# Routed rows in a two-expert layer: sorting row numbers instead of rows, fetching by them and scattering the results

## The chip, the cores and the metric

The kernel runs on one core of one Trainium2 chip. The metric is the device time of one launch in microseconds. Three runs of the kernel before took 1113.02, 1115.05 and 1116.56, median 1115.05. One more execution was profiled; all rows below are from it.

## The reference

x has 4 sequences of 1024 tokens of 256 numbers, T = 4096 tokens in all. Both branches start from the same normalised rows xn; the results are multiplied and added to x. All is float32.

```python
xn = layernorm(x)                                     # over 256
# branch 1: differential attention, 8 heads, head size 32, causal
q, k, v = xn @ wq.T, xn @ wk.T, xn @ wv.T             # q, k: two maps per head
attn = softmax(q0 k0 / sqrt(32)) - lmbda * softmax(q1 k1 / sqrt(32))
o = attn @ v                                          # per head
o = o * rsqrt(mean(o * o, over groups of 4) + 1e-6) * (1 - L_INIT)
s = o @ wo.T
# branch 2: 8 experts, the best 2 of each token
logits = xn @ router.T + router_bias
top_vals, top_idx = top_k(logits, 2);  top_w = softmax(top_vals)
gate, up = split(xn @ gate_up[e] + bias[e])           # 256 -> 2 * 256
glu = min(gate, 7) * sigmoid(1.702 * gate)
y[e] = ((clip(up, -7, 7) + 1) * glu) @ down[e] + down_bias[e]
g = silu(sum over the 2 experts of top_w * y[e])
out = x + s * g
```

## The kernel before

The program has four stages, each a block in which every engine runs its own list of instructions; at the exit of a block all five engines meet. The order inside a list is written out by hand, and engines wait on counting semaphores.

*Projections.* Eight chunks of 512 tokens. DVE normalises, PE turns the rows and makes q, k (as high and low parts, `PARTS`, stored by SP to `q_parts` and `k_parts`, L313), v and the logits. POOL makes constants at the start: masks, identity, a tile of zeros (L264), counters (L269 to L281); PE's and DVE's lists wait for `consts_done` 6. SP writes the zeros to `xs_dram` in eight DMAs (L303). DVE ranks the logits of each batch and, after the last, works out the routing (L497 to L548): a scan over the 32 tiles of tokens (six doublings, L503 to L507), the tokens and tiles of each expert, the first slot of each, the expert of each of 72 slot tiles (`expert_rows`), the slot of each token's two choices (`slot_of`) and their weights. The steps of `low_parts` (L433) stand between those of the routing in DVE's list.

*Attention.* 16 iterations of two heads, each eight frames (p = 0 to 7) of a long and a short block of queries. PE scores, DVE takes maxima and combines the two maps (L1050, L1100), ACT takes exponentials and copies. SP loads the q and k of the next head while the present one is scored (L782, L162, L163) and, in iterations 0 to 7, the weights of one expert. POOL copies v (L813), keeps the results (`keep_rows`, L826; two frames of slack to ACT) and sorts the experts' inputs: it loads two tiles of xn rows an iteration (L832), copies their slots (L833) and scatters each tile twice to `xs_dram` (L844), 1 KB a row, and waits for the scatters at the iteration's end. Rows of the slots that no token has stay zero.

*Experts.* 72 tiles of 128 slots, all buffers double. SP loads a tile of `xs_dram` when PE has turned the tile two before (L1184). In step n PE does the gate and up product of tile n+1 (L1242), turns the input of n+2 (L1228), does the down product of n-1 (L1268) and turns the activation of n (L1255). DVE adds the bias (L1359), limits the gate (L1369), multiplies (L1378), limits up (L1381), makes `act_in` (L1387) and the output `ys` (L1399). ACT copies and takes tanh, and stores `ys` plainly to `ys_dram` (L1330). POOL has nothing to do.

*Last stage.* Eight chunks of 512 tokens (b, h). POOL copies a chunk's slots and weights and gathers its 8 tiles of `ys_dram` rows (L1507, 4 tiles times 2 choices) into `yg`. ACT squares the attention results (L1571), scales the first choice (L1580, waits for the gathers), takes root and tanh (L1589, L1594). DVE in `normalise` copies a divisor (L1631), sums squares, adds the second choice (L1653), inverts the root (L1659) and scales to `On` (L1672); in `finish` of the chunk before it multiplies and adds (L1678, L1684, L1688). PE turns `On` and multiplies by wo (L1544, L1553). SP loads x and stores the result.

## Time and profile before

| | |
|---|---|
| median of 3 runs | 1115.05 us |
| the profiled execution | 1113.86 us, span 1112.0 us |
| PE, DVE, ACT, POOL busy | 941.5, 938.0, 776.8, 221.7 us |
| mean granted clock of PE | 0.949 |
| DMA | 178.11 MB, mean 160 GB/s |
| read from and written to HBM | 108.56 and 69.21 MB |

The span runs from the first to the last instruction; what the execution has around it is 1.9 us. Busy times overlap. An engine that is busy the whole of a stage sets its pace; where none is, a chain of waits does, and then the row of the instruction that is waited for tells more than the sum. A row of the timeline gives start, duration, engine, line, operation, output from inputs and, in brackets, how long the engine had stood idle and what released it.

### The profile page before, as it was taken

How to read it: one execution, taken by the hardware profiler on the slowest of the kernel's cores; microseconds unless marked ns; L12 is line 12 of the kernel's file. 1: busy time of each engine (PE TensorE's matmuls, PEld its weight loads, DVE VectorE, ACT ScalarE, POOL GpSimd, SP SyncE). 2: the span in 40 equal slices, each digit the busy share in tenths (PEclk: the TensorE clock that was granted, in tenths of full speed). 3: DMA queues.
4: the chain of work that ended last, by engine and by line, in shares of the span. 5: the costliest groups of instructions: out<-in, count | busy, mean ns of one | idle time of the engine just before them, and what ended most of it. 6: DMA issues, size and time to landing. Idle time of an engine off the chain costs nothing. (4 is left out here: it accounts for less than half of the span.)

```text
span 1112.0 us, 25771 instructions
## 1 busy us (share of the span) xinstructions
PE 941.5 (85%) x6626; PEld 659.5 (59%) x6627; DVE 938.0 (84%) x1873; ACT 776.8 (70%) x1982; POOL 221.7 (20%) x427
## 2 busy tenths in 40 slices
PE   5999858989889998988999898858999999962665
PEld 4787645666666666666666666644555555532544
DVE  6778688999999999999999999935777777754987
ACT  3554438999999999999999999942333333325663
POOL 2000001222222232222322232210000000017771
PEclk9999987999999999999999999988999999996677
DMA  7999986676786767757575665402222222223553
GB/s 258 377 366 370 328 318 137 172 183 149 172 199 165 175 157 187 184 128 165 120 159 130 139 151 128 95 15 66 80 84 77 85 80 80 80 94 96 174 182 107
DMA packets 92410, 178.11 MB, mean 160 GB/s; under 512 B 11744, under 2 KB 50144, under 8 KB 91360
## 3 DMA queue, kind: packets, MB, share of 16 engines
q1 hardware_dynamic: 74336, 147.38, 49.1%
q0 software_dynamic: 7680, 20.98, 6.5%
q10 hardware_dynamic: 10368, 9.44, 2.5%
q8 instruction: 11, 0.18, 0.1%
q14 instruction: 15, 0.12, 0.0%
HBM read 108.56 MB, written 69.21 MB: 160 GB/s over the span
## 5 line engine op out<-in xcount | busy, mean ns | idle before, releaser
L1050 DVE TENSOR_REDUCE nmax<-bank 128x1 f32<-128x1024 f32 (+3 forms) x256 | 260.4, 1017 | 4.0 <-PE bank L882 4.0
L983 ACT ACTIVATE Pr_long<-bank,nmax 128x1024 f32<-128x1024 f32 (+3 forms) x256 | 252.0, 984 | 12.2 <-DVE nmax L1050 12.1
L1010 ACT COPY AT<-bank 128x512 f32<-128x512 f32 (+3 forms) x384 | 177.0, 493 | 4.4 <-PE bank L921 2.5
L880 PE MATMUL bank<-Ks_first,Qs_first 128*128 128x512 f32 (+3 forms) x384 | 124.1, 413 | 31.1 <-ACT Pr_short L997 19.8
L1242 PE MATMUL bank<-gu_sb,xsT 128*128 x288 | 140.7, 612 | 4.8 <-DVE hid L1359 0.5
L997 ACT ACTIVATE Pr_short<-bank,nmax 128x128 f32<-128x128 f32 (+3 forms) x256 | 138.3, 540 | 8.9 <-DVE nmax L1068 1.6
L921 PE MATMUL bank<-ident,Pr_long 128*128 128x128 f32 x832 | 127.9, 281 | 18.1 <-DVE Pr_long L1100 18.1
L1100 DVE SCALAR_TENSOR_TENSOR Pr_long<-Pr_long,coef 128x1024 f32<-128x1024 f32 (+3 forms) x128 | 137.6, 1075 | 0.0
L880 PE MATMUL bank<-Ks_second,Qs_second 128*128 128x512 f32 (+3 forms) x384 | 119.4, 400 | 18.7 <-ACT Pr_short L997 18.4
L882 PE MATMUL bank<-maskb,identb 128*128 128x128 bf16 x512 | 118.1, 233 | 0.0
L921 PEld LDWEIGHTS bank<-ident,Pr_long 128*128 128x128 f32 x832 | 90.8, 143 | 31.7 <-issue 27.6
L944 PE MATMUL bank<-AT,Vj 128*32 128x128 f32 x2304 | 109.4, 279 | 0.0
L826 POOL COPY VO<-Ob 128x64 f32 (+1 forms) x128 | 30.3, 237 | 390.5 <-ACT Ob L1019 390.3
L662 PE MATMUL bank<-XNT_parts,wqk_parts 128*128 128x512 f32 x384 | 94.3, 403 | 9.7 <-DVE PARTS L433 8.3
L880 PEld LDWEIGHTS bank<-Ks_first,Qs_first 128*128 128x128 f32 x384 | 66.4, 202 | 59.3 <-ACT Pr_short L997 39.6
L880 PEld LDWEIGHTS bank<-Ks_second,Qs_second 128*128 128x128 f32 x384 | 63.5, 193 | 47.5 <-ACT Pr_short L997 39.1
L662 PEld LDWEIGHTS bank<-XNT_parts,wqk_parts 128*128 128x128 f32 x384 | 73.0, 193 | 29.5 <-issue 7.6
L882 PEld LDWEIGHTS bank<-maskb,identb 128*128 128x128 bf16 x512 | 49.9, 98 | 67.7 <-issue 49.8
L1359 DVE TENSOR_TENSOR hid<-bank,gub_sb 128x512 f32<-128x512 f32 x72 | 49.8, 692 | 35.9 <-PE bank L1242 34.3
L944 PEld LDWEIGHTS bank<-AT,Vj 128*32 128x32 f32 x2304 | 74.7, 110 | 8.8 <-issue 0.2
L1068 DVE TENSOR_REDUCE nmax<-bank 128x1 f32<-128x512 f32 (+1 forms) x128 | 79.0, 617 | 0.8 <-PE bank L882 0.6
L1242 PEld LDWEIGHTS bank<-gu_sb,xsT 128*128 128x128 f32 x288 | 49.8, 193 | 49.2 <-issue 49.2
(147 smaller groups left out, 1647.0 us busy)
## 6 DMA issues: line engine op xcount, KB each, us to landing
q_parts<-PARTS SPq DMA_DIRECT2D x32, 512.0 KB, 5.9
k_parts<-PARTS SPq DMA_DIRECT2D x32, 512.0 KB, 5.9
Qs_first<-q_parts SPq DMA_DIRECT2D x64, 256.0 KB, 6.2
Ks_first<-k_parts SPq DMA_DIRECT2D x64, 256.0 KB, 7.1
Qs_second<-q_parts SPq DMA_DIRECT2D x64, 256.0 KB, 5.9
Ks_second<-k_parts SPq DMA_DIRECT2D x64, 256.0 KB, 6.7
xs_dram<-zeros SPq DMA_DIRECT2D x8, 1152.0 KB, 8.4
xs<-xs_dram SPq DMA_DIRECT2D x72, 128.0 KB, 2.0
```

What stands on the lines that cost most here:

```text
L662: last = nc.tensor.matmul(qkbank[i % 4], wqk_parts[:, w, c, i * P:(i + 1) * P], XNT_parts[:, r, c, :], start=((c, w, r) == products[0]), s ...
L880: nc.tensor.matmul(at[:, c0:c1], Qs[head][:, m, q * P:(q + 1) * P], Ks[head][:, m, c0:c1], start=True, stop=(c1 < N))
L882: return nc.tensor.matmul(at[:, N - P:N], identb[:], maskb[:], start=False, stop=True)
L921: last = nc.tensor.transpose(tb[u % BANKS][:, i * P:(i + 1) * P], probs[:, 0, kb * P:(kb + 1) * P], ident[:])
L944: last = nc.tensor.matmul(ob[DH * g:DH * (g + 1), 0:P], Vj[head][:, kb, :], AT[unit(p, k) % 6][:, i * P:(i + 1) * P], start=first, stop=final,
L983: nc.scalar.activation(long_probs(p)[:, m, 0:N], long_slot[m][:, 0:N], ACT.Exp, bias=nmax[:, 4 * p + m:4 * p + m + 1], scale=1.0, accum_ou ...
L997: nc.scalar.activation(short_probs(p)[:, m, 0:N], short_at(p, m)[:, 0:N], ACT.Exp, bias=nmax[:, 4 * p + 2 + m:4 * p + 3 + m], scale=1.0, a ...
L1010: nc.scalar.copy(AT[u % 6][:, 0:w], tb[u % BANKS][:, 0:w]).then_inc(unit_out, 1)
L1050: nc.vector.tensor_reduce(nmax[:, 4 * p + m:4 * p + m + 1], long_slot[m][:, 0:N], AX.X, ALU.max, negate=True).then_inc(long_maxed, 1)
L1068: nc.vector.tensor_reduce(nmax[:, 4 * p + 2 + m:4 * p + 3 + m], short_slot[:, 0:N], AX.X, ALU.max, negate=True).then_inc(short_maxed, 1)
L1100: nc.vector.scalar_tensor_tensor(out=probs[:, 0, 0:N], in0=probs[:, 1, 0:N], scalar=coef[:, 2 * p + 1:2 * p + 2], in1=probs[:, 0, 0:N], op ...
L1242: last = nc.tensor.matmul(hbank[u], xsT[u][:, c, :], gu_sb[:, c, bass.ds(e, 1), :].rearrange("p o n -> p (o n)"), start=(c == 0), stop=(c ...
```

## The change

Nothing that is computed changes. Instead of the 1 KB rows, the numbers of the rows are sorted. `row_ids` holds for token t and choice k the number t + 4096 k. In eight attention iterations POOL scatters these numbers, each repeated to 64 bytes, to `ids_dram` at the token's slot; slots that nobody has hold numbers from 8192 up. SP then reads one word of each slot into `slot_rows`, and POOL makes `slot_tokens` from them (the number less 4096 once or twice). In the expert stage POOL fetches the rows of each slot tile from `xn_dram` by `slot_tokens` and scatters each result tile to `y_dram` by `slot_rows`, which lays them in token order, one plane a choice; empty slots go to 256 rows behind. SP and ACT do nothing for these transfers any more. The last stage reads `y_dram` plainly. The first tile of rows is fetched in the last attention iteration, the second at the start of the expert block, where two plain loads stand for the two first credits of `ys`.

Part of the routing moves: DVE copies the two PSUM results to SBUF (`pre`, `tot`), counts the tokens of an expert by one reduce instead of by the scan, and the scan and the slots become 14 counted steps on POOL in the first attention iteration (`route`, frames 0 to 4). Their tiles lie in the bias tile `gub_sb`, so SP waits for them before it loads the third expert. DVE's last two low parts stand before the experts' rows now. All four blocks are opened with `no_gpsimd_drain=True`.

```diff
+AHEAD = 5
...
-SORT_AT = {1: (0, 0), 2: (0, 1), 3: (1, 0), 4: (1, 1)}
+Y_ROWS = TOP_K * T + 2 * P
+ID_WORDS = 16
+SORT_ITS = T // P * TOP_K // NP
+SORT_AT = {1: (0, 1), 2: (2,), 3: (3, 4), 4: (5,), 5: (6, 7)}
...
-        xs_dram = nc.dram_tensor("xs_dram", (SLOT_TILES * P, D), F32, kind="Internal").ap()
-        ys_dram = nc.dram_tensor("ys_dram", (SLOT_TILES * P, D), F32, kind="Internal").ap()
+        ids_dram = nc.dram_tensor("ids_dram", (SLOT_TILES * P, ID_WORDS), I32, kind="Internal").ap()
+        y_dram = nc.dram_tensor("y_dram", (Y_ROWS, D), F32, kind="Internal").ap()
...
+        FREE_EXPERTS = 2
+        spare = gub_sb[:, FREE_EXPERTS:, :].rearrange("p e n -> p (e n)")
...
-            with nc.Block() as block:
+            with nc.Block(no_gpsimd_drain=True) as block:
...
-                    nc.gpsimd.memset(zeros[:], 0.0).then_inc(zeros_ready, 1)
-                    nc.gpsimd.memset(before[:], 1.0).then_inc(const_step, 1)
+                    nc.gpsimd.iota(no_rows[:], pattern=[[1, 2 * P], [0, ID_WORDS]], base=TOP_K * T, channel_multiplier=0
+                                   ).then_inc(no_rows_ready, 1)
+                    nc.gpsimd.iota(row_ids[:], pattern=[[P, NT], [T, TOP_K]], base=0, channel_multiplier=1
+                                   ).then_inc(no_rows_ready, 1)
...
-                    sp.wait_ge(zeros_ready, 1)
-                    xs_v = xs_dram.rearrange("(n p r) d -> n p (r d)", p=P, r=SLOT_TILES // NCH)
+                    sp.wait_ge(no_rows_ready, 1)
+                    sp.dma_start(ids_dram.rearrange("(q n) o -> q n o", n=2 * P), no_rows[:]).then_inc(ids_cleared, 16)
                     def chunk(b, h):
-                        sp.dma_start(xs_v[b * 2 + h], zeros[:]).then_inc(zeros_stored, 16)
...
+                    nc.vector.tensor_copy(pre, bank6[:, 0:NT * E].rearrange("p (t e) -> p t e", e=E))
+                    nc.vector.tensor_copy(tot, bank7[:, 0:NT * E].rearrange("p (t e) -> p t e", e=E))
...
-                    nc.vector.memset(run[0][:, 0:1, :], 0.0)
-                    then(nc.vector.tensor_copy(run[0][:, 1:NT, :], tot[:, 0:NT - 1, :]))
-                    src, span = 0, 1
-                    while span < NT:
-                        nc.vector.tensor_copy(run[1 - src][:, 0:span, :], run[src][:, 0:span, :])
-                        then(nc.vector.tensor_tensor(run[1 - src][:, span:, :], run[src][:, span:, :],
-                                                     run[src][:, 0:NT - span, :], ALU.add))
-                        src, span = 1 - src, 2 * span
...
+                    then(nc.vector.tensor_reduce(tokens, bank7[:, 0:NT * E].rearrange("p (t e) -> p e t", e=E), AX.X,
+                                                 ALU.add))
                     low_parts(B - 1, 1, range(QKT // 2, QKT // 2 + 2))
...
+                    nc.vector.tensor_scalar(first_slot, first, float(P), None, ALU.mult)
+                    low_parts(B - 1, 1, range(QKT // 2 + 2, QKT))
...
-                    low_parts(B - 1, 1, range(QKT // 2 + 2, QKT))
-                    then(nc.vector.tensor_tensor(run[1 - src][:], run[src][:], pre, ALU.add))
-                    then(nc.vector.tensor_tensor(run[src][:], run[1 - src][:],
-                                                 first_slot.unsqueeze(1).broadcast_to([P, NT, E]), ALU.add))
-                    for k in range(TOP_K):
-                        then(nc.vector.tensor_tensor(ck[:, k], chosen[:, k], run[src][:], ALU.mult))
-                    then(nc.vector.tensor_reduce(top[:, 3:5], ck, AX.X, ALU.add))
-                    then(nc.vector.tensor_copy(slot_of[:].rearrange("p t k -> p k t"), top[:, 3:5]))
...
-                    with sp.Fori(0, E) as it:
+                    with sp.Fori(0, FREE_EXPERTS) as it:
                         for u in range(2):
                             load(it + 1, u)
                         load_expert(it)
-                    with sp.Fori(E, NIT - 1) as it:
+                    sp.wait_ge(routed, ROUTE_OPS)
+                    with sp.Fori(FREE_EXPERTS, E) as it:
+                        for u in range(2):
+                            load(it + 1, u)
+                        load_expert(it)
+                    with sp.Fori(E, SORT_ITS + 2) as it:
+                        for u in range(2):
+                            load(it + 1, u)
+                    sp.wait_ge(ids_sorted, 16 * SORT_ITS * NP)
+                    with nc.allow_non_contiguous_dma("one word of each slot"):
+                        sp.dma_start(slot_rows[:], ids_dram[:, 0:1].rearrange("(n p) o -> p (n o)", p=P)
+                                     ).then_inc(rows_known, 16)
+                    with sp.Fori(SORT_ITS + 2, NIT - 1) as it:
                         for u in range(2):
                             load(it + 1, u)
...
+                    def double(src, span):
+                        nc.gpsimd.tensor_copy(run[1 - src][:, 0:span, :], run[src][:, 0:span, :])
+                        then(nc.gpsimd.tensor_tensor(run[1 - src][:, span:, :], run[src][:, span:, :],
+                                                     run[src][:, 0:NT - span, :], ALU.add))
...
+                    def sort_ids(it, p):
+                        if p == 0:
+                            if not isinstance(it, int):
+                                pool.wait_ge(ids_sorted, 16 * NP * (it - 1))
+                            tiles = bass.ds((it - 1) * (NP // 2), NP // 2)
+                            nc.gpsimd.tensor_copy(sort_slot[:], slot_of[:, tiles, :]).then_inc(row_slot_ready, 1)
+                            nc.gpsimd.tensor_copy(sort_id, row_ids[:, tiles, :].unsqueeze(3).broadcast_to(
+                                [P, NP // 2, TOP_K, ID_WORDS])).then_inc(row_slot_ready, 1)
+                        if p == 1:
+                            pool.wait_ge(row_slot_ready, 2 * it)
                             pool.sem_inc(scatter_begun, 1)
-                        pool.indirect_dma_start(xs_dram, bass.IndirectOffsetOnAxis(row_slot[u][:, k:k + 1], 0),
-                                                rows[u][:], None).then_inc(rows_sorted[u], 16)
+                        for n in SORT_AT.get(p, ()):
+                            i, k = n // TOP_K, n % TOP_K
+                            pool.indirect_dma_start(ids_dram, bass.IndirectOffsetOnAxis(sort_slot[:, i, k:k + 1], 0),
+                                                    sort_id[:, i, k, :], None).then_inc(ids_sorted, 16)
+                    def tokens_of_slots():
+                    def tokens_of_slots():
+                        pool.wait_ge(rows_known, 16)
+                        for i, (row, token) in enumerate(((slot_rows, slot_tokens), (slot_tokens, slot_tokens))):
+                            past = xs_first[:, 0:SLOT_TILES].bitcast(I32)
+                            nc.gpsimd.tensor_scalar(past, row[:], T, T, ALU.is_ge, ALU.mult).then_inc(tokens_step, 1)
+                            pool.wait_ge(tokens_step, 2 * i + 1)
+                            nc.gpsimd.tensor_tensor(token[:], row[:], past, ALU.subtract).then_inc(tokens_step, 1)
+                            pool.wait_ge(tokens_step, 2 * i + 2)
...
-                        for u in range(2):
-                            pool.wait_ge(rows_sorted[u], 32 * (it + 1))
+                    def nothing(it, p):
+                        pass
+                    def first_rows(it, p):
+                        if p == 1:
+                            tokens_of_slots()
+                            pool.indirect_dma_start(xs_first[:], None, xn_dram, bass.IndirectOffsetOnAxis(
+                                slot_tokens[:, 0:1], 0)).then_inc(xs_loaded[0], 16)
                     pool.sem_inc(o_kept, NP)
-                    iteration(0)
-                    with pool.Fori(1, NIT) as it:
-                        iteration(it)
+                    iteration(0, lambda it, p: route(p))
+                    iteration(1, sort_ids)
+                    with pool.Fori(2, SORT_ITS + 1) as it:
+                        iteration(it, sort_ids)
+                    with pool.Fori(SORT_ITS + 1, NIT - 1) as it:
+                        iteration(it, nothing)
+                    iteration(NIT - 1, first_rows)
...
-            with nc.Block() as block:
-                xs_v = xs_dram.rearrange("(n u p) d -> n u p d", u=2, p=P)
-                ys_v = ys_dram.rearrange("(n u p) d -> n u p d", u=2, p=P)
-                @block.sync
-                def _(sp):
-                    def load(it, u):
-                        sp.wait_ge(xs_turned, seen(it, u - 2))
-                        sp.dma_start(xs[u][:], xs_v[it, u]).then_inc(xs_loaded[u], 16)
-                    with sp.Fori(0, NIT3) as it:
-                        for u in range(2):
-                            load(it, u)
+            with nc.Block(no_gpsimd_drain=True) as block:
+                @block.gpsimd
+                def _(pool):
+                    def rows_in(n):
+                        pool.wait_ge(xs_turned, seen(n // 2 - 1, n % 2))
+                        pool.indirect_dma_start(xs[n % 2][:], None, xn_dram, bass.IndirectOffsetOnAxis(
+                            slot_tokens[:, n:n + 1], 0)).then_inc(xs_loaded[n % 2], 16)
+                    def results_out(n):
+                        pool.wait_ge(y_ready, seen(n // 2, n % 2))
+                        pool.indirect_dma_start(y_dram, bass.IndirectOffsetOnAxis(slot_rows[:, n:n + 1], 0),
+                                                ys[n % 2][:], None).then_inc(y_stored[n % 2], 16)
+                    pool.indirect_dma_start(xs[1][:], None, xn_dram, bass.IndirectOffsetOnAxis(
+                        slot_tokens[:, 1:2], 0)).then_inc(xs_loaded[1], 16)
+                    for u in range(2):
+                        pool.dma_start(ys[u][:], xn_dram[0:P, :]).then_inc(y_stored[u], 16)
+                    for n in range(2, AHEAD):
+                        rows_in(n)
+                    for n in range(SLOT_TILES):
+                        if n + AHEAD < SLOT_TILES:
+                            rows_in(n + AHEAD)
+                        results_out(n)
+                    for u in range(2):
+                        pool.wait_ge(y_stored[u], 16 * (NIT3 + 1))
...
-                def store(it, n):
-                    if not there(it, n):
-                        return
-                    it, u = it + n // 2, n % 2
-                    nc.scalar.wait_ge(y_ready, seen(it, u))
-                    nc.scalar.dma_start(ys_v[it, u], ys[u][:]).then_inc(y_stored[u], 16)
...
+                    y_v = y_dram[0:TOP_K * T, :].rearrange("(k b h t p) d -> k b h p t d", k=TOP_K, b=B, h=2, p=P)
+                    def load_y(b, h):
+                        for k in range(TOP_K):
+                            sp.dma_start(yg[h][:, :, k, :], y_v[k, b, h]).then_inc(y_loaded[h], 16)
...
+                            sp.wait_ge(ff_ready, credited(b, 2, h))
+                            load_y(b + 1, h)
                             store(b, h)
...
-                            nc.gpsimd.tensor_copy(yslot[h][:], slot_of[:, bass.ds(c, CT), :]).then_inc(picked, 1)
                             nc.gpsimd.tensor_copy(yw[h][:], weight[:, bass.ds(c, CT), :]).then_inc(picked, 1)
-                            pool.wait_ge(picked, credited(b, 4, 2 * h + 1))
-                            pool.sem_inc(gather_begun, 1)
-                            for i in range(CT):
-                                for k in range(TOP_K):
-                                    pool.indirect_dma_start(
-                                        yg[h][:, i, k, :], None, ys_dram,
-                                        bass.IndirectOffsetOnAxis(yslot[h][:, i, k:k + 1], 0)
-                                    ).then_inc(y_gathered[h], 16)
                 def outputs(b, h):
```

## Rows read from the trace of the kernel before

**Rows 1.** The page's slices: busy tenths of POOL in 40 slices of 27.8 us.
```profile
POOL 2000001222222232222322232210000000017771
```

**Rows 2.** Windows by stage: length, busy us of each engine, granted clock, DMA share, GB/s.
```profile
161.60:741.40 579.80, 518.83 (x4992) 371.02 (x4992) 560.15 (x960) 558.24 (x1537) 145.40 (x320) 0.98 0.65 150
...
751.90:995.40 243.50, 232.12 (x864) 137.17 (x864) 174.02 (x432) 83.47 (x216) 0.00 (x0) 0.99 0.24 77
995.40:1112.00 116.60, 60.48 (x192) 46.74 (x192) 83.33 (x136) 62.71 (x88) 69.68 (x80) 0.69 0.47 144
```

**Rows 3.** Groups by line of the last stage: busy us, mean ns | idle before, releaser.
```profile
L1507 POOL DMA_INDIRECT yg<-ys_dram,yslot x64 | 65.3, 1021 | 23.6 <-issue 17.1 <-POOL yw L1501 6.6
```

**Rows 4.** Timeline of the last stage: start, duration, instruction, idle before.
```profile
1009.06 1.70 ACT L1580 ACTIVATE ff<-yg,yw 128x256 f32<-128x256 f32 x4 [12.16 <-DMA yg<-ys_dram,yslot]
...
1031.17 0.17 DVE L1631 COPY d1x<-d_all 128x32 f32 x1
...
1041.88 0.17 DVE L1631 COPY d1x<-d_all 128x32 f32 x1
...
1096.70 1.43 DVE L1672 TENSOR_TENSOR On<-VO,root 128x256 f32<-128x256 f32 x4
```

**Rows 5.** Timeline between attention and experts.
```profile
749.86 13.65 SPq L1184 DMA_DIRECT2D xs<-xs_dram  x6
...
751.98 1.19 PE L1228 MATMUL bank<-ident,xs 128*128 128x128 f32 x4 [11.32 <-DMA xs<-xs_dram]
```

**Rows 6.** Line 775, the attention block: duration min/median/max in ns, start.
```profile
L775 POOLq DRAIN  x1: 8172/8172/8172, 741.1 to 741.1; - x1
```

**Rows 7.** Timeline of the start.
```profile
5.14 2.01 POOL L264 MEMSET zeros<- 128x2304 f32 x1
...
6.47 1.08 DVE L357 TENSOR_SCALAR ve<-mv 128x4 f32<-128x4 f32 x1
...
7.49 0.18 POOL L269 IOTA count_i<- 128x72 int32 x1
...
10.41 1.94 PE L647 MATMUL bank<-ident,XN 128*128 128x128 f32 x8 [10.41 <-DVE XN L381]
```

**Rows 8.** Timeline of the end of the projections.
```profile
151.69 0.60 ACT L594 ACTIVATE PARTS<-bank 128x512 fp32r<-128x512 f32 x1 [0.76 <-PE bank L662]
...
155.78 1.29 DVE L433 SCALAR_TENSOR_TENSOR PARTS<-bank,PARTS 128x512 fp32r<-128x512 f32 x2
...
160.79 0.15 DVE L553 TENSOR_SCALAR lam_s<-lam_s 128x1 f32<-128x1 f32 x1
161.62 0.34 SPq L162 DMA_DIRECT2D Qs_second<-q_parts  x1
```

**Rows 9.** The page's DMA queues: packets, MB, share of 16 engines.
```profile
q10 hardware_dynamic: 10368, 9.44, 2.5%
```

**Rows 10.** The page's DMA issues: count, KB each, median us to landing.
```profile
xr<-x SPq DMA_DIRECT2D x8, 512.0 KB, 3.6
...
xs_dram<-rows,row_slot POOLq DMA_INDIRECT x64, 3.0
...
yg<-ys_dram,yslot POOLq DMA_INDIRECT x64, 2.8
```

**Rows 11.** Timeline of the expert stage, one period.
```profile
861.26 0.29 DVE L1369 TENSOR_SCALAR hid<-hid 128x256 f32<-128x256 f32 x1
861.31 0.38 PE L1255 MATMUL bank<-ident,act_in 128*128 128x128 f32 x2
...
862.98 0.42 DVE L1387 SCALAR_TENSOR_TENSOR act_in<-up,glu 128x256 f32<-128x256 f32 x1 [0.20 <-DVE up L1381]
...
864.38 0.38 PE L1255 MATMUL bank<-ident,act_in 128*128 128x128 f32 x2
```

**Rows 12.** Timeline of the last stage, an indirect DMA begun during a DVE step.
```profile
1062.27 1.22 DVE L1678 SCALAR_TENSOR_TENSOR ft<-ft,ff 128x1024 f32<-128x1024 f32 x1
...
1062.82 1.50 POOL L1507 DMA_INDIRECT yg<-ys_dram,yslot  x1 [0.30 <-issue]
```

More of the change, by code:

```diff
@@ L510, in _ @@
+                    then(nc.vector.tensor_reduce(tokens, bank7[:, 0:NT * E].rearrange("p (t e) -> p e t", e=E), AX.X,
+                                                 ALU.add))
                     low_parts(B - 1, 1, range(QKT // 2, QKT // 2 + 2))
-                    tokens, tiles, first, end, first_slot = (per_e[:, i] for i in range(5))
-                    then(nc.vector.tensor_tensor(tokens, run[src][:, NT - 1, :], tot[:, NT - 1, :], ALU.add))
-                    ce = cmp[:, 0:E * NT].rearrange("p (e t) -> p e t", e=E)
+                    ce = rcmp[:, 0:E * NT].rearrange("p (e t) -> p e t", e=E)
@@ L717, in build @@
             nmax = sb("nmax", [P, 2 * NQ], where=ph)
-            rows = [sb(f"rows{u}", [P, D], where=ph) for u in range(2)]
-            row_slot = [sb(f"row_slot{u}", [P, TOP_K], U32, where=ph) for u in range(2)]
+            sort_slot = sb("sort_slot", [P, NP // 2, TOP_K], U32, where=ph)
+            sort_id = xs_first[:, D - NP * ID_WORDS:].bitcast(I32).rearrange(
+                "p (t k o) -> p t k o", k=TOP_K, o=ID_WORDS)
             rec = sb("rec", [P, NQ], where=ph)
@@ L1138, in build @@
         with ExitStack() as ph:
-            xs = [sb(f"xs{u}", [P, D], where=ph) for u in range(2)]
+            xs = [xs_first, sb("xs_second", [P, D], where=ph)]
             xsT = [sb(f"xsT{u}", [P, HC, P], where=ph) for u in range(2)]
```

171 lines of the change are left out of this document (102 added, 69 removed).

## The prediction

> **What bounds the kernel now.** I read the forty slices first, then the busy time by stage, then the places where a stage ends, and only then single instructions. In the slices POOL is empty at the expert stage and works at seven tenths near the end [rows 1]. By stage [rows 2]: in attention (580 us) DVE is busy 560 and ACT 558, so those two set the pace and neither POOL nor the DMA does. In the expert stage (243.5 us) PE is busy 232 and POOL 0. In the last stage (116.6 us) nothing is full: DVE 83, POOL 70, PE 60. There the page's chain that ended last runs through the 64 gathers of L1507, its largest item. A gather keeps POOL for 1.02 us and 0.30 us pass before the next [rows 3], so eight of them plus two copies and their waits make about 11.8 us a chunk. DVE alone needs less: the chunk that did not wait went from copy to copy of L1631 in 10.7 us, 1031.17 to 1041.88 [rows 4]. And between attention and experts the core stands still from 741.3 to 749.86 [rows 5], under one instruction: POOL's drain at the exit of that block, 8.17 us from 741.1 [rows 6].
>
> **The change part by part**, against the profiled execution's own time, 1113.86 us (span 1112.0).
>
> *Start, +2.8.* POOL's memset of the zeros (2304 words a partition, 2.01 us) becomes an iota of 4096 words, and a small second one follows. This is on the path. POOL's later constants gate PE, and the memset already holds DVE: L357, a TENSOR_SCALAR on 4 words, began at 6.47, inside the memset, and took 1.08 us [rows 7]; its other seven runs take 0.17. PE begins at 10.41, 2.86 after L357 ends, and the projections then run PE-bound, so what starts late ends late. The trace has one iota, 72 words in 0.18 us [rows 7]; less some 0.10 for a one-word memset that is 1.1 ns a word, so 4096 words take 4.6 us and the small one 0.17: 2.8 us more than the memset. Bounds: at the memset's 0.87 ns a word +1.7 (and if DVE's L357 slips ahead of the iota, only POOL's own constants bind, which had 1.5 us to spare: +0.2); at the 1.5 ns of a 128-wide affine select +4.3. I take the iota's own row.
> Going with it, eight DMAs of 1152 KB of zeros become one of 0.6 MB. The DMA engines are nearly full there, but ACT's and PE's waits in that stage are for one another and never for a store, so I give this nothing but the last store's landing, next.
>
> *End of the projections, -3.3.* DVE held the last two low parts back behind the routing: they started at 155.78 though ACT had delivered the last high part at 152.29, and DVE's last step ended at 160.94 [rows 8]. In the new order DVE runs two PSUM copies (0.41 each, as L503), the reduce of the counts (0.42), low parts 4 and 5 (ACT delivers 5 at 149.57), six steps of 0.17 to 0.42, and at about 152.3 low parts 6 and 7, done at 153.4 instead of 157.07. Then come 2.0 us for the experts' rows and 1.1 for weights and lambda: DVE ends near 156.7. The last store is issued near 153.5; before, 3.6 us passed from the last issue to the last landing, and with four stores closer together I give it 4.7, so 158.2, and 0.6 us for the block exit. The next stage opened at 161.62 [rows 8] and opens 3.3 earlier (2.5 to 3.8, from the landing).
>
> *Attention, 0.* What leaves DVE (the scan and the slots) goes to POOL in the first iteration, spread over five frames of 4.4 us. The largest bundle, three doublings, is six instructions of 0.3 to 0.7, about 3 us, and keep_rows has two frames of room. The 64 scatters stay 64 but carry 64 bytes a row, and fill eight iterations instead of sixteen; 32 row loads and their copies go. Since POOL has 390 us of waiting on ACT there, both ends are near 0. SP gets two waits. That for the routing is met long before. That for the sorted ids comes after the loads of iteration 10, and behind it stands a read of one word from each of 9216 rows. Those are 576 words for each of 16 DMA engines. The smallest packets of the trace, queue 10's, take 2.5% of 16 x 1112 us over 10368 packets, 43 ns each for about 1 KB [rows 9]: at most 25 us. The next head load stands behind it in the same queue. From the landing of the load before to that issue there are about 11 us, and another 7 until the load is late, 18 in all. A word is less than 1 KB, so I take it as hidden: 0, at most +7.
>
> *Into the experts, -7.2.* Without the drain the block can end at 741.3 + 0.6 = 741.9. The first tile lies in xs_first by then. PE, however, turns tiles 0 and 1 before its first product, and tile 1 is fetched only at the block's start: 0.5 us until POOL issues, 2.8 from issue to landing [rows 10], so PE turns tile 1 at 745.3. Before, the first plain load was issued at 749.86 and tile 1 was turned from 752.5, half a microsecond after tile 0 [rows 5]. That is 7.2 of the 8.17. Late next is POOL: behind the fetch it issues two plain DMAs and the fetches of tiles 2 and 3. Tile 2 lands near 748.6 and is wanted near 751.6. If both ends slip I get -6.2; if a shorter pause saves the clock its dip, -8.5.
>
> *The experts, 0.* Each tile now costs POOL one fetch and one scatter. At 1.02 + 0.30 [rows 3] that is 2.64 us beside a PE period of 3.05 (PE's steps at 861.31 and 864.38 [rows 11] are 3.07 apart). With the longer gap seen after a wait (0.66) it is 2.9 to 3.0: close to full, but a queue that falls behind stops waiting and is back at 2.64. The fetch for tile n+5 can be issued when tile n+3 is turned, 6.1 us before PE turns n+5, and lands after about 3.5; the scatter has 5.6 us until DVE wants the buffer and lands after 3.0 [rows 10] plus 0.6. So 2 us are left on either side. ACT loses its store, which PE never waited for. The other end is the first rival.
>
> *Out of the experts, +1.8.* DVE's last y is ready at 993.23 (L1399, 0.42 from 992.81). Before, the plain store and the exit took 2.2 us; now 0.6 until the scatter, 3.0 to land, 0.4 to leave: 4.0.
>
> *Last stage, -16.8.* With plain reads the first y pair (1 MB in two DMAs) lands near 5.1 us after the start (3.6 for 512 KB alone [rows 10], plus its second half), where ACT had waited 12.2 us and began at 1009.06 [rows 4]. In the old time frame: ACT starts ff(0) at 1000.6, DVE ends On(0) at 1007.3. Chunk 1 waits once more for ACT (tanh, squares, two copies, 1.70 for ff: 1011.6) and ends On(1) at 1016.5, finish(0) at 1020.2. From there ACT (7.9 us a chunk) is ahead and DVE runs at 10.8: On(2) 1027.3, On(7) 1081.3, against 1098.13 [rows 4]. What follows On(7) (PE's last 16 products, two DVE steps, the store, 13.9 us) is unchanged. Late next would be SP: load_y for h=1 is issued behind a store's landing, reaches ACT about 9.5 us after res_ready, and is wanted at 11.1. Ends: -18.5 if chunk 1's wait goes, -10.8 if every chunk keeps the 1.0 to 1.2 us that DVE now waits for ACT.
>
> Sum: 2.8 - 3.3 + 0 - 7.2 + 0 + 1.8 - 16.8 = -22.7, so 1091.2 for an execution like the profiled one. The median of the runs lies 1.2 above that execution, so I forecast 1092.
>
> **The rivals.**
> *The port, slower (13%).* POOL's indirect DMAs now run beside DVE in the expert stage, for 2.0 of each 3.05 us. Two kinds of holding stand in the trace: L357 held by a POOL memset [rows 7], and an indirect DMA that began 0.55 us into DVE's L1678, which reads two tiles, and took 1.50 instead of 0.95 [rows 12]. If an indirect DMA holds DVE's TENSOR_SCALARs as the memset did, two a tile (L1369, L1381, 0.29 each) wait up to 0.95. The place is act_in: DVE ends it at 863.41 and PE turns it at 864.38 [rows 11], so 0.97 a tile is absorbed. One hold of 0.85 costs nothing, two cost 0.73. Every second tile: 36 x 0.73 = +26, 1118; every tile +53. It decides from 22.7 / 72 = 0.32 us a tile. For it: L1369 at 861.26 falls just where a fetch triggered by the turn before would run. Against it: one L1631 copy (0.17) ran at its usual length within an indirect DMA, and no row shows a TENSOR_SCALAR beside one. The Trainium skill speaks for this rival: "SBUF — State Buffer", section "Who interferes with whom", has VectorE's two-port modes and GpSimd share a port pair that whoever issues first keeps for the whole instruction. The memset row agrees; for descriptor writing no row decides.
> *A little of the port (9%).* 0.15 a tile: 1103.
> *The last stage stays tied to ACT (11%).* 6 chunks at 1.0 more: 1098. For: L1653 waited about 1.1 us in five chunks. Against: ACT itself waited for the gathers in them.
> *The word read delays a head load (6%).* 1099. The Trainium skill's "DMA: Bandwidth & Descriptors", "Rules for kernel authors", says that a strided last dim lowers to one descriptor per element, which is this rival's premise; the trace has no such read.
> *The pause stays (4%),* because something other than the drain fills 741 to 749: 1100. Nothing speaks for it but that one drain is all the evidence.
> *More comes back (7%):* iota at the memset's pace and no clock dip: 1086.
>
> **How the numbers follow.** The forecast, 1092, has 50%, with its own range 1085 to 1099. A measurement can tell 0.3%, 3.3 us. Slower: most of the first rival, 0.12; same 0.03; faster 0.85. For 8 in 10 I leave out most of the first rival (0.12) and the best few cases (0.04): 1083 to 1112.
>
> **What would show it.** Start: PE's first transpose near 13.2, an iota of 4.6 us. No POOL drain between attention and experts and PE's pause near 4 us. Expert period 3.05, L1369 and L1381 still 0.29; if they read 0.5 or more and PE waits for act_in, the first rival holds. Last stage: no DMA_INDIRECT, L1631 to L1631 in 10.7 to 10.9, about 99 us. The forecast is wrong if the expert stage passes 250 us, if PE idles for q or k loads near iteration 11, or if the last stage stays above 105.

## The result, and the profile after

| | before | after |
|---|---|---|
| median of the runs, us | 1115.39 (1113.02 to 1116.56) | 1087.69 (1086.14 to 1088.61) |
| profiled execution, us (span) | 1113.86 (1112.0) | 1086.14 (1084.4) |

The ratio is 0.9754, 95% interval 0.9737 to 0.9771: 27.7 us faster. I had forecast 1092 (1083 to 1112), a gain of 22.7 on the profiled execution; its span fell by 27.6. The stages, each read between the same two events of both traces:

| step | forecast | measured | from, to |
|---|---|---|---|
| start | +2.8 | +1.9 | PE's first transpose 10.41, 12.35 |
| projections | -3.3 | -2.3 | until SP's first load of the next stage: 151.2, 148.9 |
| attention | 0 | -0.3 | until GpSimd's last copy: 579.7, 579.4 |
| into the experts | -7.2 | -7.7 | until PE turns tile 1: 11.1, 3.4 |
| experts | 0 | -5.4 | until DVE's last result: 240.7, 235.3 |
| out of the experts | +1.8 | +0.9 | until the first load: 2.2, 3.2 |
| last stage | -16.8 | -14.7 | until the end: 116.5, 101.9 |

One execution of each is not exact to a microsecond. Of the kernels profiled here, ten (the changed one among them) have the changed projections and attention and took 148.7 to 151.0 us, mean 149.7, for the projections; the four with the old ones 151.1 to 153.0, mean 151.7: that term is nearer to -2.0. Attention is 578.6 to 579.7, mean 578.9, in the four, and 579.3 to 582.0, mean 580.5, in the ten: about +1.6 and not 0; its cause was not looked for.

The start, in the timeline (start, duration, instruction):
```profile
5.04 4.39 POOL L291 IOTA no_rows<- 36x4096 int32 x1
...
6.39 3.07 DVE L385 TENSOR_SCALAR ve<-mv 128x4 f32<-128x4 f32 x1
...
12.35 1.94 PE L653 MATMUL bank<-ident,XN 128*128 128x128 f32 x8 [12.35 <-DVE XN L409]
```
As against [rows 7]: the iota (1.07 us per thousand words; I took 1.1) holds DVE's L385, four words, for 3.07 us until it ends itself, and PE waits for what follows. It is 0.9 less than my +2.8: the iota took 4.4 and not 4.6, the second iota is not on the path (0.17), and L357 of before ended 0.4 us behind the memset, where L385 ends with the iota.

The end of the projections, timeline:
```profile
151.37 4.89 SPq L341 DMA_DIRECT2D k_parts<-PARTS  x4
...
157.85 0.15 DVE L559 TENSOR_SCALAR lam_s<-lam_s 128x1 f32<-128x1 f32 x1
161.22 0.34 SPq L194 DMA_DIRECT2D Qs_second<-q_parts  x1
```
DVE ends at 158.0, 3 us ahead of the exit, where in [rows 8] it set it. The last store now does; and this is the stretch from 155 us to the exit in the trace's view of the DMA:
```profile
GB/s 403 351 351 390 403 403 351 299 416 390 403 403 312 364 416 390 390 390 351 390 364 403 403 416 364 312 403 403 390 325 65 0 0 0 0 0 0 0 0 0
...
k_parts<-PARTS SPq DMA_DIRECT2D x1, 512.0 KB, 5.1
```
The queues run at 299 to 416 GB/s, mostly near 400, until the store has landed. That the transfers before it make the 5.1 us where I gave 4.7 fits this; no run tests it.

Into the experts, timeline:
```profile
741.27 0.97 POOL L1283 DMA_INDIRECT xs_second<-xn_dram,slot_tokens  x1 [0.65 <-SPq L1268]
741.47 0.41 PE L1335 MATMUL bank<-ident,xs_first 128*128 128x128 f32 x2 [1.51 <-ACTq L1434]
744.03 0.69 PE L1335 MATMUL bank<-ident,xs_second 128*128 128x128 f32 x2 [2.14 <-DMA xs_second<-xn_dram,slot_tokens]
744.82 5.96 PE L1349 MATMUL bank<-gu_sb,xsT 128*128 x8
```
There is no drain, and GpSimd's first fetch comes 0.65 us after its last copy, as against [rows 5, 6].

The expert stage. All 72 instances of the two TENSOR_SCALARs (duration min/median/max in ns), and half a period:
```profile
L1463 DVE TENSOR_SCALAR hid<-hid x72: 293/294/299, 749.5 to 974.6; 128x256 f32<-128x256 f32 x72
```
```profile
L1475 DVE TENSOR_SCALAR up<-hid x72: 281/286/484, 750.6 to 975.8; 128x256 f32<-128x256 f32 x72
```
```profile
840.85 0.97 POOL L1274 DMA_INDIRECT xs_first<-xn_dram,slot_tokens  x1 [0.50 <-PE bank L1335]
841.23 0.29 DVE L1463 TENSOR_SCALAR hid<-hid 128x256 f32<-128x256 f32 x1
...
842.29 0.99 POOL L1280 DMA_INDIRECT y_dram<-ys,slot_rows  x1 [0.47 <-DVE ys L1493]
...
842.78 0.29 DVE L1475 TENSOR_SCALAR up<-hid 128x256 f32<-128x256 f32 x1
```
Both lie inside an indirect DMA and keep their 0.29 us. Of the 72 of each, 66 and 70 overlap one; a single L1475 took 0.48. The first rival is dead. GpSimd waits for PE or DVE before each DMA, so it keeps up.

The word read, issued at 522.81, in the view of DMA issues (count, KB, us to landing), and SP's next head load behind it:
```profile
slot_rows<-ids_dram SPq DMA_DIRECT2D x1, 36.0 KB, 13.6
```
```profile
536.67 0.33 SPq L194 DMA_DIRECT2D Qs_first<-q_parts  x1
```
The head loads keep their step of 17.7 us (501.28, 518.96, 536.67): hidden.

The last stage, timeline, as against [rows 4]:
```profile
982.53 0.97 SPq L1567 DMA_DIRECT2D yg<-y_dram  x2
...
988.09 1.70 ACT L1671 ACTIVATE ff<-yg,yw 128x256 f32<-128x256 f32 x4 [4.13 <-DMA yg<-y_dram]
...
1030.33 0.17 DVE L1722 COPY d1x<-d_all 128x32 f32 x1
...
1034.30 1.75 DVE L1750 RECIPROCAL root<-root 128x256 f32<-128x256 f32 x1 [0.18 <-ACT root L1680]
...
1041.27 0.17 DVE L1722 COPY d1x<-d_all 128x32 f32 x1
...
1047.27 1.43 DVE L1763 TENSOR_TENSOR On<-VO,root 128x256 f32<-128x256 f32 x4 [0.27 <-DVE root L1750]
```
ACT starts 5.6 us into the stage (5.1 forecast), and a chunk takes 10.94 or 11.25 us in turn, mean 11.06 from 1008.14 to 1063.45.

### The profile page after: what moved, and what is told of

Read it like the earlier page. It is cut to its first block and busy times, and to the rows that moved or that the text cites. A ratio compares the mean times of both kernels' runs of the same rounds, so it can differ in the third digit from the quotient of the medians.

```text
span 1084.4 us, 25051 instructions
## 1 busy us (share of the span) xinstructions
PE 932.2 (86%) x6626; PEld 652.0 (60%) x6627; DVE 938.8 (87%) x1857; ACT 769.4 (71%) x1982; POOL 284.1 (26%) x478
## 5 line engine op out<-in xcount | busy, mean ns | idle before, releaser
L1406 ACT COPY xsT<-bank 128x256 f32<-128x256 f32 x72 | 26.8, 372 | 112.6 <-PE bank L1335 112.6
L1280 POOL DMA_INDIRECT y_dram<-ys,slot_rows x72 | 71.4, 992 | 41.7 <-DVE ys L1493 40.4
```

## The experiments

The question was the expert stage: -5.4 us where I had 0. A word on the table: "pair" is the mean time of two tiles between 790 and 950 us (one turn of the loop), "turn" what passes between the start of PE's turning of act_in, the last of the loop's body, and the gate product behind it; in the middle of the body the same two instructions are 0.22 us apart.

| kernel | median, us | pair | turn | act_T ends before the gate product by |
|---|---|---|---|---|
| before | 1115.4 | 6.48 | 0.50 | 1.61 |
| e3, no drain | 1104.45 | 6.37 | 0.45 | 1.62 |
| e2, store behind | 1104.13 | 6.23 | 0.31 | 2.30 |
| e9, both | 1097.26 | 6.20 | 0.27 | 2.26 |
| after | 1087.69 | 6.37 | 0.45 | 2.44 |
| e1, wait back | 1089.80 | 6.38 | 0.46 | 2.12 |
| e4, drains back | 1096.72 | 6.38 | 0.46 | 2.44 |
| e10, plain rows | 1086.74 (one run) | 6.35 | 0.43 | 2.42 |
| e11, no GpSimd | 1081.73 (one run) | 6.20 | 0.28 | 2.26 |

**e1**, the changed kernel with ACT's wait of before:
```diff
                         gate_curve(it, n + 1)
+                        if there(it, n - 1):
+                            nc.scalar.wait_ge(y_ready, seen(it + (n - 1) // 2, (n - 1) % 2))
                         act_out(it, n)
```


> The changed kernel with one wait put back in the expert stage: before act_out of tile n ACT waits again until DVE has written the results of tile n-1, as it did when it issued their store. No DMA is added. The changed kernel runs this stage 5.4 us faster than I forecast (a pair of tiles in 6.36 us where it took 6.49). Theory W (PE's down products waited for act_T, which stood behind that wait in ACT's queue): the pair goes back to 6.49, 36 pairs by 0.13 = +4.7 us, so about 1092.3. Rival D (it was ACT's issue of the store, 0.34 us a tile, or the queue that it used): no change, or at most half, 1087.7 to 1090. Rival S (it was SP's plain loads of xs beside PE): no change, 1087.7.

Ratio to before 0.9765 (0.975 to 0.978), the pair 6.38. Theory W fails as I put it: the wait alone puts act_T off by some 0.3 us, and the pair does not grow. The ratio's interval touches that of the changed kernel (0.9737 to 0.9771), so the 2.1 us between the medians are no clear difference.

**e2**, the kernel before with two calls exchanged:
```diff
-                        store(it, n - 1)
                         act_out(it, n)
+                        store(it, n - 1)
```


> The kernel before with two calls of ACT's step in the expert stage exchanged: act_out of tile n first, then the store of tile n-1 with its wait. Theory W: the expert stage gets the 4.7 us without anything else of the change, so about 1110.5 against 1115.2, and the pair of tiles takes 6.36. Rivals D and S: the issue of the store and SP's loads are still there, so the pair stays at 6.49 and the time at 1115.

0.9904 (0.9889 to 0.9919): 11.3 us faster, more than twice what W had. The pair is 6.23, shorter than in the changed kernel. PE and ACT in e2's timeline:
```profile
849.97 0.35 ACT L1321 COPY act_T<-bank 128x256 f32<-128x256 f32 x1
850.39 0.34 ACTq L1330 DMA_DIRECT2D ys_dram<-ys  x1
...
852.31 0.38 PE L1255 MATMUL bank<-ident,act_in 128*128 128x128 f32 x2
852.65 1.98 PE L1242 MATMUL bank<-gu_sb,xsT 128*128 x4
```
And the same in the kernel before, beside [rows 11]:
```profile
849.46 0.34 ACTq L1330 DMA_DIRECT2D ys_dram<-ys  x1
...
849.95 0.37 ACT L1321 COPY act_T<-bank 128x256 f32<-128x256 f32 x1 [0.82 <-DVE ys L1399]
...
851.43 0.38 PE L1255 MATMUL bank<-ident,act_in 128*128 128x128 f32 x2
851.95 1.98 PE L1242 MATMUL bank<-gu_sb,xsT 128*128 x4
```
So ACT's order of act_T and store costs the old loop 0.25 us a pair; e2 shows that with no other edit. The path that I read from the rows is a ring: gate product, DVE's hid, ys, ACT's wait with the store behind it (0.5 us), act_T, PE's down product, the turn, the gate product. PE shows hardly any idle time in it. That its sequencer, late from the wait for act_T, is late at the turn is my reading of 0.50 against 0.31; the profile does not show the sequencer. The sign is the last column, 1.61 and 1.62 us in the two kernels that have the ring and anything above 2 in the others. In e1 act_T ends 2.12 us ahead, 0.50 more than in the ring, though it has the same wait: it lacks the issue. So it seems to take wait and issue together to hold PE. No run put both back into the changed kernel.

**e3**, the kernel before without any drain (`nc.Block()` becomes `nc.Block(no_gpsimd_drain=True)` four times).

> The kernel before, all four blocks without the drain of GpSimd at their exit, nothing else. If the drain is all that holds the core between attention and experts, 7.6 us go there (8.17 less 0.6 for the exit) and nothing elsewhere, since in the other blocks GpSimd has long been idle or ends far ahead of the others: about 1107.5. If the pause stays for another reason: 1115.

0.9911 (0.9894 to 0.9928), 10.9 us faster. Tile 0 is turned 8.1 us earlier after GpSimd's last copy. The rest was not expected: the pair is 6.37, and DVE begins the odd tile's ys 0.12 us earlier in the ring (3.30 after the gate product at the turn instead of 3.42), which is about the 0.11 that the pair lost. Before and e2 have 3.42, all the others 3.30; DVE waits there for nothing that the trace shows. Why stays open. The last stage gave 3.5 us back (120.0 against 116.5), and as much in e9: in both one chunk takes 14.6 us from copy to copy of L1631 where before it took 10.71.

**e4**, the changed kernel with four drains.

> The changed kernel with the drains put back in all four blocks. Between attention and experts +7.6 us. At the end of the experts GpSimd now works until the last scatter has landed, which it did not before; if its drain takes 8 us there too, +8 more: about 1103.5. If a drain is dear only behind the work of the attention stage (it took 8.17 us there), the second costs under 1 us: 1095.5. The other two are beside other work: 0.

0.9841 (0.9826 to 0.9856), 1096.72: +9.0, between my two figures. The exits of attention and of the experts in e4:
```profile
L785 POOLq DRAIN  x1: 5637/5637/5637, 740.9 to 740.9; - x1
```
```profile
L1268 POOLq DRAIN  x1: 2912/2912/2912, 988.7 to 988.7; - x1
```
A drain has no fixed price (8.17 in [rows 6]), and behind the experts' 145 DMAs it is the shortest of the three. Counted within this change, leaving them out is worth 5.7 us into the experts and 2.9 out of them. The pair stays at 6.38 with the drains back: in the changed kernel the gain in the loop is not the drains', as it was in e3.

**e9**, e2 and e3 together.

> The kernel before with the store behind act_out and without the drains (e2 and e3 together); GpSimd does nothing in the expert stage. If the two edits are separate, 1115.4 less 8.1 for the pause and 9.9 for the shorter pair of tiles, about 1097, with the pair at 6.23 us as in e2. Theory G (the changed kernel stays at 6.37 because GpSimd's fetches run beside PE's turn of the loop, where PE loads its expert numbers from SBUF): 6.23 here, since there are none. Theory L (the length of the loop's turn follows the place of the code, which the drains move by one instruction): 6.37 here, as in every kernel so far that had no drain, and about 1102.

0.984 (0.982 to 0.9861), 1097.26 against a forecast of 1097. The pair is 6.20: theory L falls. With act_T out of the way and GpSimd idle, the loop is at 6.20.

**e10**, the changed kernel with SP's plain loads in place of the fetches, and **e11**, ACT's plain stores in place of the scatters as well:
```diff
-                            rows_in(n + AHEAD)
+                        sp.dma_start(xs[u][:], xn_v[0, u]).then_inc(xs_plain[u], 16)
...
-                        results_out(n)
+                    nc.scalar.dma_start(y_dram[u * P:(u + 1) * P, :], ys[u][:]).then_inc(y_stored[u], 16)
```


> The changed kernel with its fetches in the expert stage replaced by plain loads that SP issues, under the same waits; the scatters of the results stay. It leaves out the sorting: every tile after the first gets the first rows of xn, so its output isn't the reference's. Theory G: the pair of tiles goes from 6.37 to 6.23 us. Theory L, or a cause in the scatters: it stays at 6.37.

> The changed kernel with neither of GpSimd's indirect DMAs in the expert stage: rows by SP's plain loads as in e10, results by ACT's plain store behind act_out as in e9. It leaves out sorting and scattering, so its output isn't the reference's. PE's program in the stage is that of the changed kernel. Without GpSimd the kernel of e9 took 6.20 us for a pair of tiles, the changed kernel takes 6.37, with plain loads alone 6.35. Theory G (the scatter, or either of the two, holds PE's turn of the loop by 0.15 us): 6.20 here, the turn 0.28. Theory L (it goes with the program and its place, not with what GpSimd does): 6.35 here, the turn 0.44.

The pairs are 6.35 and 6.20. PE's turn in e10, with the scatter ahead of it, then in e11:
```profile
853.05 0.96 POOL L1281 DMA_INDIRECT y_dram<-ys,slot_rows  x1 [2.46 <-DVE ys L1502]
...
854.97 0.38 PE L1371 MATMUL bank<-ident,act_in 128*128 128x128 f32 x2
855.43 1.98 PE L1358 MATMUL bank<-gu_sb,xsT 128*128 x4
```
```profile
853.83 0.38 PE L1371 MATMUL bank<-ident,act_in 128*128 128x128 f32 x2
854.13 1.98 PE L1358 MATMUL bank<-gu_sb,xsT 128*128 x4
```
PE's work in the stage is the same in both. With GpSimd's scatters in place of ACT's plain stores the turn is 0.15 us longer (mean 0.43 against 0.28), and the fetches on top add 0.02 at most. The fetches without the scatters were not run. What in a scatter does it is open: its instruction ends at 854.01, 0.96 us before the turn begins, so it is not that instruction running beside PE's turn; the scatter lands only about 0.5 us into the turn, where a plain store of e11 has landed 0.5 us ahead of it. A turn of 0.45 needs no scatter either: e3 has it from the ring. So against the old loop the order of act_T and the store, with the drains, is worth 0.28 us a pair (e9), and 0.17 comes back with the scatters and fetches: 35 pairs by 0.11 are 3.9 of the 5.4. Most of the rest is the emptying of the loop, where PE waits for act_T: the last three results came 2.67 us apart and now 2.2 and 1.9.

**e6**, the control for the first rival:
```diff
+                        nc.gpsimd.memset(busy[:], 0.0).then_inc(busy_done, 1)
                         pool.wait_ge(y_ready, seen(n // 2, n % 2))
```


> The changed kernel with a memset of 1024 words a partition on GpSimd ahead of the scatter of every tile: the control for my first rival. In the profile of the changed kernel L1463 and L1475 keep their 0.29 us inside the indirect DMAs of GpSimd, so writing descriptors does not hold them. If an elementwise operation of GpSimd does (as the memset and the iota at the start held a TENSOR_SCALAR), the memset, about 1 us a tile, meets L1463 or L1475 in each tile; one of the two then reads 0.5 us or more and the pair grows: 0 to 0.7 us a tile, 1088 to 1138. If it is only GpSimd's own time that counts (2.6 us a tile of indirect DMAs and now 3.7 beside a tile of 3.19), the tile takes 3.7 with both TENSOR_SCALARs still at 0.29: about 1124.

0.9944 (0.9924 to 0.9965), 1108.97: +21.3, 0.30 a tile. Timeline, and all 72 of two DVE steps:
```profile
850.69 0.97 POOL L1282 MEMSET busy<- 128x1024 f32 x1
850.75 1.06 DVE L1480 TENSOR_SCALAR up<-hid 128x256 f32<-128x256 f32 x1
...
851.83 1.00 POOL L1284 DMA_INDIRECT y_dram<-ys,slot_rows  x1 [0.17 <-issue]
...
853.13 1.07 POOL L1276 DMA_INDIRECT xs_first<-xn_dram,slot_tokens  x1 [0.30 <-issue]
...
853.70 1.98 PE L1354 MATMUL bank<-gu_sb,xsT 128*128 x4 [0.69 <-DVE hid L1458]
...
854.20 0.97 POOL L1282 MEMSET busy<- 128x1024 f32 x1
```
```profile
L1480 DVE TENSOR_SCALAR up<-hid x72: 285/882/1368, 753.5 to 1000.4; 128x256 f32<-128x256 f32 x72
```
```profile
L1477 DVE SCALAR_TENSOR_TENSOR glu<-gate_tanh,hid x72: 424/426/427, 753.2 to 1000.0; 128x256 f32<-128x256 f32 x72
```
The TENSOR_SCALAR is held. Of the 72 SCALAR_TENSOR_TENSORs 63 were running when a memset began and one began inside a memset; neither they nor the memsets took longer. So a GpSimd instruction can hold this DVE step, and an indirect DMA does not.

The 0.30 us a tile, however, is not the price of such a hold by itself. Between 790 and 950 us GpSimd never waits for another engine: memset, scatter and fetch with 0.17 and 0.30 us between them take 3.5 us a tile, which is the pace of the stage (a pair takes 6.96). GpSimd is full, and the hold ties DVE, and through it PE (0.69 us behind DVE's hid in every pair), to GpSimd's pace. What a hold costs beside a GpSimd that has time to spare, as in my rival, this run doesn't show. By the Trainium skill's "SBUF — State Buffer", section "Who interferes with whom", that is what is to be seen: a TENSOR_SCALAR may take both port pairs, a step with two SBUF inputs meets only a GpSimd step that reads. The traces agree, here and in e7.

**e7**, the last addition of each chunk on GpSimd:
```diff
-                        nc.vector.tensor_tensor(xr[h][:], ft[h][:], xr[h][:], ALU.add).then_inc(res_ready, 1)
+                        nc.gpsimd.tensor_tensor(xr[h][:], ft[h][:], xr[h][:], ALU.add).then_inc(res_ready, 1)
```


> The changed kernel with the last addition of each chunk (L1779, 1.23 us of DVE) moved to GpSimd, which is idle in the last stage. ACT's wait before the first expert's result is then for the silu step, which frees that buffer. If DVE alone sets the chunk (my reading of the last stage: 10.9 to 11.25 us from copy to copy of L1722), it falls to 9.7 to 10.0: eight times 1.2 less the 1.5 us that GpSimd is slower at the very end, about -8, 1079.7. If the chunk is tied to ACT (ff, root, tanh, squares, two copies: 7.9 us of work in DVE's order) DVE waits for root instead, and half of it or less comes: 1083 to 1086. If GpSimd's addition holds DVE as its memset held L1475 in e6, it is nothing: 1088.

0.9803 (0.9788 to 0.9819), 1093.04: 5.3 us slower than the changed kernel, which none of my three figures had. 3.2 of it lie in the last stage, where the mean chunk is 11.27 us; the rest lies in stages that the edit does not touch. Timeline:
```profile
1033.44 2.41 POOL L1606 TENSOR_TENSOR xr<-ft,xr 128x1024 f32<-128x1024 f32 x1 [9.56 <-DVE ft L1789]
1033.59 1.22 DVE L1745 TENSOR_REDUCE square_sum<-sq 128x256 f32<-128x1024 f32 x1
1034.10 1.71 ACT L1685 ACTIVATE ff<-yg,yw 128x256 f32<-128x256 f32 x4 [1.54 <-DMA yg<-y_dram]
1034.92 1.22 DVE L1750 SCALAR_TENSOR_TENSOR square_sum<-d1e,square_sum 128x256 f32<-128x256 f32 x1
...
1036.01 0.40 SPq L1575 DMA_DIRECT2D out<-xr  x1
```
GpSimd's addition takes 2.4 us where DVE's took 1.23, and in three chunks of eight it holds L1750, a DVE step of 0.43 us, until it ends (the reduce beside it is not held). And SP's queue pays: the store waits for the slower addition, and with it the next loads. From the third chunk on ACT waits for yg in four chunks of six, in the changed kernel in one.

**e8**, PE's first gate product ahead of turning tile 1:
```diff
                     turn_rows(0, 0)
-                    turn_rows(0, 1)
                     load = expert_loader(pe)
                     gate_and_up(0, 0, load(0))
+                    turn_rows(0, 1)
```


> The changed kernel; at the start of the expert stage PE multiplies tile 0 by the gate weights before it turns tile 1, for whose fetch it waits 2.14 us now. The products of tile 0 then run in that wait: the stage ends up to 2.1 us earlier, 1085.6. If the order costs as much elsewhere (ACT copies tile 1 ahead of tile 0's tanh; a colder clock in the products), nothing: 1087.7.

0.9759 (0.9746 to 0.9773), 1088.98: nothing gained. The stage's first stretch (length, busy PE and so on, granted clock, DMA share) in the changed kernel and in e8, up to the third gate product:
```profile
741.47:752.37 10.90, 7.71 (x17) 3.27 (x17) 2.94 (x7) 1.53 (x4) 4.92 (x6) 0.69 0.21 60
```
```profile
743.46:754.02 10.56, 9.24 (x16) 3.88 (x17) 2.92 (x7) 1.53 (x4) 4.33 (x6) 0.52 0.23 62
```
The wait is filled, but all eight products then run at 0.94 us each, at 1.2 GHz (granted clock 0.52 over the stretch), 7.5 us in all, where the changed kernel took 5.96 for the eight (0.69). The stretch ends 0.3 us earlier and not 2.1.

**e5** and **e12**, the start, and a loop with four tiles in its body:
```diff
-nc.gpsimd.iota(no_rows[:], pattern=[[1, 2 * P], [0, ID_WORDS]], base=TOP_K * T, channel_multiplier=0
+nc.gpsimd.iota(no_rows[:], pattern=[[0, SLOT_TILES // 2], [1, 2], [0, ID_WORDS]], base=TOP_K * T, channel_multiplier=2
```


> The changed kernel with the row numbers of the empty slots laid over all 128 partitions instead of 36: the iota has 1152 words a partition instead of 4096, the same 0.6 MB go out in pieces of 128 bytes. The iota takes 4.39 us now; at the same pace a word it takes 1.3, ends at 6.35, and DVE's L385 no longer stands behind it. PE's first transpose comes 2.9 us earlier, at 9.4 instead of 12.35, and the whole follows, since the projections are bound by PE: about 1084.8. If the start is bound by the loads of x and the weights instead, PE begins no earlier than before the change, 10.4: 1085.7. If the small pieces delay the loads of the projections, it is nothing or worse: 1088 or more.

0.973 (0.9712 to 0.9748), 1084.79 as forecast, 2.9 less than the changed kernel and the fastest of all that compute the whole (e11, which leaves work out, took 1081.73). Timeline:
```profile
5.04 1.42 POOL L291 IOTA no_rows<- 128x1152 int32 x1
...
6.30 0.19 DVE L386 TENSOR_SCALAR ve<-mv 128x4 f32<-128x4 f32 x1
```
L385 of the changed kernel, here L386, is free again, and PE starts at 9.39.

```diff
-                    with eng.Fori(0, NIT3 - 2) as it:
-                        e = load(it)
-                        step(it, 1, e)
-                        step(it, 2, e)
+                    with eng.Fori(0, (NIT3 - 2) // 2) as half:
+                        e = [load(half * 2 + j, j) for j in range(2)]
+                        for j in range(2):
+                            step(half * 2 + j, 1, e[j])
+                            step(half * 2 + j, 2, e[j])
```


> The kernel of e5 (wide iota) with the expert loop's body doubled: 17 turns of four tiles instead of 34 of two, with the expert numbers of all four loaded at the top. At a turn PE stands 0.46 us before the gate product where it stands 0.22 in the middle of the body. If that is the price of the branch, 17 turns fewer save 17 x 0.24 = 4.1 us: about 1080.7 against e5's 1084.8. If it is the price of loading expert numbers, which now happens twice in a row at each turn, the turn grows to some 0.7 and nothing is saved: 1084.8; if the longer program costs fetches, it is slower than e5.

0.9767 (0.9748 to 0.9786), 1087.76: slower than e5.
```profile
840.82 0.38 PE L1365 MATMUL bank<-ident,act_in 128*128 128x128 f32 x2
841.84 1.98 PE L1352 MATMUL bank<-gu_sb,xsT 128*128 x4 [0.64 <-issue]
```
The turn is 1.02 us here and 0.95 in most: a second set of expert numbers costs 0.5 us more, which is more than the whole turn of one set has beyond the 0.22 inside the body. So the loading of registers from SBUF is dear; what the branch alone costs was not measured. It is not a longer program being fetched at each turn: the page counts 12 and 19 packets on the two instruction queues in the whole of e12, and 11 and 18 in e5, for 17 turns. Four tiles take 12.91 us where two turns took 12.74, and 17 by 0.17 is the 2.9 us that e12 lost on e5.

## Why the prediction was right, and where it was not

*Right in direction and mechanism.* The order of the terms stands: last stage, then the drain, then small change at both ends. The pause fell to 3.4 us (near 4 forecast), with e3 and e4 to show that it was the drain; the last stage is without gathers and DVE-bound; the word read is hidden.

*The experts, 0: the step that failed.* I wrote "ACT loses its store, which PE never waited for". PE did wait for it, by act_T, though PE was busy 232 of 243.5 us and inside the loop no idle time of PE named ACT. I had priced only one side of that store, its issue, and not the wait ahead of it in the same queue. e2 shows what it cost: 11.3 us of the kernel before go when act_T stands ahead of the store. That the total still came near the forecast is luck in part: the gain of the ring (e2, e9) is larger than what came, because PE's turn is longer with GpSimd's scatters (e10, e11), a cost that no rival of mine had; and the -5.4 here and the last stage's 2.1 have opposite signs.

*The last stage, -16.8: mis-sized by 2.1.* ACT began 0.5 late (the first pair of DMAs had landed 5.5 us after the stage opened), and a chunk took 11.06 instead of 10.8. Of the rival "tied to ACT" a small part is true, 0.2 of its 1.0 us a chunk: DVE waits 0.18 to 0.24 us for ACT's root in each chunk. In every second one it waits 0.27 more at L1763, for its own L1750 by the trace. The chunk of [rows 4] from which I took 10.7 had neither wait: one chunk is a thin base for a term that counts six times.

*Start and end of the projections* partly cancelled, as forecast, each a microsecond less than forecast. *Out of the experts* +0.9: a scatter lands in 2.4 to 2.6 us and not in 3.0.

*The first rival* (13%) hung on one thing alone, what GpSimd does beside DVE. Its premise failed: an indirect DMA holds no TENSOR_SCALAR. e6 shows the hold with a memset. Its 21 us are near the 26 I had written only by chance, since there GpSimd's own 3.5 us a tile set the pace.

## What to carry to other kernels

Before an engine's store is called free, follow what stands behind it in the same queue, its wait above all: a loop can be a ring through a queue although every engine in it looks either full or idle. The sign is a constant delay between one event and another across kernels, and the test is cheap: exchange two calls (e2 gave 11.3 us on the old kernel with no other edit). GpSimd's indirect DMAs left DVE's steps alone, but elementwise work of GpSimd did not: its memset held a TENSOR_SCALAR, its addition a two-input step. And before an engine is given more per tile, add up its own instructions and gaps: in e6 they came to the pace of the stage.

## What was not expected of the hardware

- With GpSimd's scatters in the loop PE's turn, at which it loads four registers from SBUF, is 0.43 to 0.46 us, with plain stores 0.28 (e10 and after, e11); the scatter's instruction has ended 0.96 us before. A second set of registers costs 0.5 us more (e12). That it is the loading which the scatters slow is not shown.
- A GpSimd drain took 8.17, 5.64 and 2.91 us, behind 96, 65 and 145 DMAs of its block: not in the order of their number.
- DVE begins the odd tile's ys 0.12 us later in two kernels (before and e2) than in all the others; nothing in the trace says why.
